# Six fields looked up through one-hot matrices instead of four, in a recommendation tower on one core

## The reference, cut to what matters

```
e = jnp.stack([tbl_0[ids[:, 0]], ..., tbl_31[ids[:, 31]]], axis=1)      # 2048 x 32 x 64
rows, cols = np.triu_indices(32, k=1)                                   # 496 pairs of fields
p, q = e[:, rows, :], e[:, cols, :]
pij = jnp.einsum('bpe,dpe,bpd->bp', p, kernel, q)                       # kernel: 64 x 496 x 64
z = pij @ W.T + b                                                       # 256
h = jnp.concatenate([z, dense_ctx], axis=1)                             # 272
h = jnp.maximum(h @ W_top1 + b_top1, 0.0)                               # 512
h = jnp.maximum(h @ W_top2 + b_top2, 0.0)                               # 256
y = h @ W_top3                                                          # 1
```

## Time and profile before

| what | us |
|---|---|
| median of 3 runs | 860.19 (859.13 to 860.83) |
| the profiled execution, whole | 859.6 |
| its span, from first to last instruction | 857.8 |
| PE busy in the span | 829.0 |
| DVE busy | 616.9 |
| ACT busy | 560.7 |
| POOL busy, all in the first 640 us | 472.2 |

### The profile page before, as it was taken

One profiled execution on the slowest core, in us unless ns is written; L12 is line 12 of the kernel. 1 busy time (PEld: TensorE's weight loads), 2 busy tenths in 40 slices (PEclk: granted clock), 3 DMA queues, 4 the chain that ended last, 5 costly groups with the idle time before them and its releaser, 6 DMA issues.

```text
span 857.8 us, 14292 instructions
## 1 busy us (share of the span) xinstructions
PE 829.0 (97%) x4104; PEld 289.5 (34%) x4104; DVE 616.9 (72%) x577; ACT 560.7 (65%) x4181; POOL 472.2 (55%) x502
## 2 busy tenths in 40 slices
PE   4999899999999999999999999999999999999998
PEld 1433233333333333333333333333333333333333
DVE  4478688888765766988765666888866775888850
ACT  0114698898716778898714777888822776888941
POOL 5777777777777777777777777777720000000000
PEclk9999999999999999999999999999999999999999
DMA  9911111111111111111111111111100000000000
GB/s 259 351 37 27 27 27 29 28 27 28 28 28 28 27 27 27 27 29 28 27 29 27 27 28 28 28 27 28 27 15 0 1 1 1 2 1 1 1 2 0
DMA packets 21621, 29.78 MB, mean 35 GB/s; under 512 B 10898, under 2 KB 11410, under 8 KB 20904
## 3 DMA queue, kind: packets, MB, share of 16 engines
q0 software_dynamic: 15872, 16.28, 9.8%
q1 hardware_dynamic: 3512, 9.84, 3.2%
q10 hardware_dynamic: 2160, 2.76, 1.2%
HBM read 28.85 MB, written 0.01 MB: 34 GB/s over the span
## 4 chain that ended last, share of the span: by engine, by line
PE 82%; POOL 7%; issue 5%; DVE 3%; ACT 2%; DMA 0%; DVEq 0%; SPq 0%; POOLq 0%
PE bilinear L692 36%; PE sums L732 19%; PE bilinear L704 13%; PE sums L763 8%; POOL emb_first L440 4%; POOL emb L440 3%; PE bilinear L670 3%; PE bilinear L763 2%; ACT batch_prod L525 1%; DVE batch_prod L603 1%; DVE prod L589 1%; DVE prod L592 1%; DVE prod L587 1%; DMA emb<-table,ids_sb 0%; DMA sums_sb<-dense_t 0%
## 5 line engine op out<-in xcount | busy, mean ns | idle before, releaser
L525 ACT ACTIVATE batch_prod<-batch_prod 128x64 f32<-128x64 f32 x2048 | 490.5, 241 | 98.9 <-DVE batch_prod L603 98.5
L592 DVE TENSOR_TENSOR prod<-bilinear,emb_t 128x1024 f32<-128x1024 f32 x352 | 414.9, 1216 | 123.2 <-PE bilinear L692 113.3
L440 POOL DMA_INDIRECT emb<-table,ids_sb x368 | 347.3, 944 | 112.2 <-issue 110.3
L692 PE MATMUL bilinear<-emb_t,k_sb 64*128 64x512 f32 x1536 | 389.4, 614 | 2.9 <-DVE prod L592 0.9
L525 ACT ACTIVATION_READ_ACCUMULATOR batch_prod<-batch_prod 128x1 f32 x2048 | 383.1, 187 | 0.0
L692 PEld LDWEIGHTS bilinear<-emb_t,k_sb 64*128 64x128 f32 x1536 | 131.4, 186 | 240.9 <-issue 115.5
L603 DVE TENSOR_TENSOR batch_prod<-bilinear,emb_first 128x1024 f32<-128x1024 f32 x128 | 155.7, 1216 | 46.3 <-PE bilinear L704 46.3
L732 PE MATMUL sums<-prod,pair_sel 128*32 128x512 f32 x1472 | 180.3, 600 | 1.1 <-DVE prod L589 1.1
L440 POOL DMA_INDIRECT emb_first<-table,ids_sb x128 | 124.2, 971 | 44.9 <-issue 37.3
L704 PE MATMUL bilinear<-k_sb,emb_t 64*128 64x512 f32 x512 | 138.2, 616 | 1.5 <-DVE prod L589 0.7
L484 ACT ACTIVATE emb_t<-bilinear 128x1024 f32<-128x1024 f32 (+1 forms) x40 | 33.8, 844 | 88.2 <-PE bilinear L670 81.5
(11 more groups left out here) (39 smaller groups left out, 139.6 us busy)
## 6 DMA issues: line engine op xcount, KB each, us to landing
emb<-table,ids_sb POOLq DMA_INDIRECT x368, 2.4
k_sb<-k_slots SPq DMA_DIRECT2D x2, 1088.0 KB, 21.6
emb_first<-table,ids_sb POOLq DMA_INDIRECT x128, 2.4
k_sb<-k_slots SPq DMA_DIRECT2D x1, 1600.0 KB, 23.0
k_sb<-k_slots SPq DMA_DIRECT2D x1, 1472.0 KB, 19.6
sums_sb<-looked_ids SPq DMA_DIRECT2D x1, 1024.0 KB, 10.2
k_sb<-k_slots SPq DMA_DIRECT2D x1, 960.0 KB, 14.8
k_sb<-k_slots SPq DMA_DIRECT2D x1, 896.0 KB, 24.8
```

Source lines behind the costliest of these rows:

```text
L440: nc.gpsimd.indirect_dma_start(fields_of(i, j, t)[:, f % 2, :], None, tables[f], bass.IndirectOffsetOnAxis(ap=ids_sb[:, start + t, f:f + 1 ...
L525: last = nc.scalar.activation(products, products, ACT.Copy, accum_out=batch_sums[:, t, row + f:row + f + 1])
L592: last = nc.vector.tensor_tensor(prod[:, at:at + 2, 0:n], bilinear[:, bank:bank + 2, 0:n], emb_t[:, j:j + 1, 0:n].to_broadcast([P, 2, n]), ...
L692: last = nc.tensor.matmul(bilinear[:, bank + row // EMB, 0:n], k_sb[row:row + EMB, operand, :], emb_t[row:row + EMB, double, 0:n], start=T ...
```

## The change

Three doubles instead of two are looked up in chunk 0, made of the six fields with 1000-row tables, in 3 x 8 steps of 125 rows. The ids of these fields are copied to all partitions in three parts of two fields each, with a semaphore each; the third part is put where the gathers of chunk 1 write later (`emb_first`, slot 1). SP waits for the first part before it issues the operands. DVE waits for each part ahead of the steps that read it. POOL waits for all 24 one-hot steps ahead of the gathers of chunk 1. The ids come from the host in an order in which each partition's ids lie together, so that the first copy moves 128 runs of 512 bytes, not 512 runs of 128. `BATCH_DOUBLES` moves from doubles 2 to 5 to doubles 3 to 6 and `BATCHED_ROWS_OF` from 6 to 13 to 7 to 14. The spacing of the batches changes.

```
-LOOKED_UP = 2
-LOOKED_FIELDS = (8, 9, 12, 13)
-TABLE_ROWS = (1250, 1000, 1000, 1250)
+LOOKED_UP = 3
+LOOKED_FIELDS = (1, 9, 12, 20, 22, 25)
+TABLE_ROWS = 1000
...
-TABLE_STEPS = 10
-TABLE_PARTS = tuple(rows // TABLE_STEPS for rows in TABLE_ROWS)
+TABLE_STEPS = 8
+TABLE_PARTS = TABLE_ROWS // TABLE_STEPS
...
-BATCH_DOUBLES = range(2, 6)
+BATCH_DOUBLES = range(3, 7)
...
-BATCHED_ROWS_OF = range(6, 14)
+BATCHED_ROWS_OF = range(7, 15)
...
-FIRST_BATCH_FROM, FIRST_BATCH_EVERY = 18, 2.4
-BATCH_FROM, BATCH_EVERY = 12, 2.45
+FIRST_BATCH_FROM, FIRST_BATCH_EVERY = 24, 2.2
+BATCH_FROM, BATCH_EVERY = 18, 2.3
...
-        looked_ids_sb = sums_sb[:, 0:2 * LOOKED_UP, :].bitcast(i32)
+        looked_ids_sb = [sums_sb[:, 2 * j:2 * j + 2, :].bitcast(i32) for j in range(LOOKED_UP - 1)]
+        looked_ids_sb.append(emb_first[:, 1, 0:2, :, :].rearrange("p a f e -> p a (f e)").bitcast(i32))
...
-            ids_by_tile = ids.rearrange("(t p) f -> p t f", p=P)
             first = CHUNK_TILES[0]
-            sp.dma_start(ids_sb[:, 0:first, :], ids_by_tile[:, 0:first, :]).then_inc(s_ids[0], 16)
-            sp.dma_start(looked_ids_sb, looked_ids.partition_broadcast(P)).then_inc(s_looked_ids, 16)
+            sp.dma_start(ids_sb[:, 0:first, :], ids[:, 0:first, :]).then_inc(s_ids[0], 16)
+            for j in range(LOOKED_UP):
+                sp.dma_start(looked_ids_sb[j],
+                             looked_ids[2 * j:2 * j + 2, :].partition_broadcast(P)).then_inc(s_looked_ids[j], 16)
+
+            sp.wait_ge(s_looked_ids[0], 16)
             for piece in range(len(K_PIECES)):
...
                     pool.wait_ge(s_ids[1], 16)
+
+                    pool.wait_ge(s_one_hot, LOOKED_UP * TABLE_STEPS)
...
-            dve.wait_ge(s_looked_ids, 16)
             for j in range(LOOKED_UP):
+                dve.wait_ge(s_looked_ids[j], 16)
                 for k in range(TABLE_STEPS):
...
-                    nc.vector.tensor_scalar(one_hot[:, at:at + 2, :], looked_ids_sb[:, 2 * j:2 * j + 2, :],
+                    nc.vector.tensor_scalar(one_hot[:, at:at + 2, :], looked_ids_sb[j],
                                             rows_sb[:, k:k + 1], None, ALU.is_equal).then_inc(s_one_hot, 1)
...
-    ids = give("ids", np.asarray(inputs["ids"])[:, FIELDS])
+    ids = give("ids", np.asarray(inputs["ids"])[:, FIELDS].reshape(BATCH // P, P, NUM_FIELDS).transpose(1, 0, 2))
```

More of the change, by code:

```diff
@@ L334, in build @@
         s_table = [sem(f"s_table{f}") for f in range(2 * LOOKED_UP)]
-        s_looked_ids = sem("s_looked_ids")
+        s_looked_ids = [sem(f"s_looked_ids{j}") for j in range(LOOKED_UP)]
         s_rows = sem("s_rows")
@@ L401, in _ @@
                 if piece == 0:
-                    sp.dma_start(ids_sb[:, first:, :], ids_by_tile[:, first:, :]).then_inc(s_ids[1], 16)
+                    sp.dma_start(ids_sb[:, first:, :], ids[:, first:, :]).then_inc(s_ids[1], 16)
             for i in range(NCHUNKS):
@@ L451, in _ @@
             for f in range(2 * LOOKED_UP):
-                act.dma_start(tables_sb[0:TABLE_PARTS[f], f, :, :],
+                act.dma_start(tables_sb[0:TABLE_PARTS, f, :, :],
                               tables[f].rearrange("(p k) e -> p k e", k=TABLE_STEPS)).then_inc(s_table[f], 16)
@@ L623, in look_up @@
                             pe.wait_ge(s_table[f], 16)
-                        parts = TABLE_PARTS[f]
-                        last = nc.tensor.matmul(bilinear[c * EMB:(c + 1) * EMB, bank, :], tables_sb[0:parts, f, k, :],
-                                                one_hot[0:parts, n % ONE_HOT_RING * 2 + c, :],
+                        last = nc.tensor.matmul(bilinear[c * EMB:(c + 1) * EMB, bank, :], tables_sb[0:TABLE_PARTS, f, k, :],
+                                                one_hot[0:TABLE_PARTS, n % ONE_HOT_RING * 2 + c, :],
                                                 start=k == 0, stop=k == TABLE_STEPS - 1, tile_position=(0, c * EMB))
```

## The result

The changed kernel takes **877.86 us** in the median of four runs (875.50 to 878.21), against 859.66 for the kernel before beside it: a ratio of 1.021, 95% interval 1.0196 to 1.0225. The forecast was 855.3 us and the range ended at 858.3. The profiled execution took 878.21 us, with a span of 876.4.

A forecast was written before the change was run, and what follows sets the result against it. PE was taken to bound later chunks, leaving gains in the first 97 us: start -0.2, first turn -0.56, double 9 -4.5, double 7 -0.3, spacing +0.7, in sum -4.9 us, so 855.3 us; range 851.3 to 858.3.

The follow-up runs named there:

- e13: Changed kernel, tables in one transfer each, but SP issues the other ids and the operands behind its first piece only when all six tables have landed: 852.83 us.
- e5: Changed kernel with each table copied by two transfers, of 112 and 13 partitions, and nothing else changed: 859.78 us, 1.0003 of the kernel before.
- e11: e5 with SP issuing the operands only behind all three parts of the ids, DVE still beginning behind the first part: 851.50 us, .9909 of the kernel before.
- e12: e5 with SP issuing the operands only when the fold's factors have landed: 854.47 us, .9933 of the kernel before.
- e6: Changed kernel with each table copied by two transfers, of 124 and 1 rows: 880.16 us, 1.0247 of the kernel before.

## What to carry to other kernels

Before sums are made with a queue's pace, divide each transfer's bytes by the engines that its partition count allows: by that rule 125 partitions use five, and cut into 112 + 13 the waits for them fell from 18.1 to 1.3 us. And make the same edit in the kernel that you compare with. A wait that moves a large transfer has two sides: ask not only whether it still comes in time, but what then runs beside it on the same engines, on every queue. And what is behind the start can be judged by itself: here the time from first slot to end was 805.5 or 805.6 us in eight kernels whose first slots lay up to 28.5 us apart.

## What the runs showed of the hardware

- Six tables of 250 KB in one transfer each, issued from 0.7 us on, had all landed by 25.9 us with the operands held back (e13), and by 48.4 with the operands beside them (the changed kernel).
- The layout of one queue's transfers moved those of another: the first 512 KB of ids landed at 6.2 to 6.8 us with the tables cut 112 + 13 (e5, e11, e12) and at 10.3 with 124 + 1 (e6).
- A 2 KB transfer issued at 8.61 us landed at 40.0 us (e5), where the DMA share was 1.03 from 8 to 40 us; its size didn't tell when it would come.
- The fold at the end of a busy look-up was granted 1.00 in e11 and e13, 0.52 from 36 to 40 us in e12, with the same 0.78 us of rest ahead of it; the fold was 3.1 us longer for it.
- In the first steps of the look-up the matmuls run at half their later pace while the granted clock reads 1.00 (12 to 17 us of the kernel before).
